# First cross attention with the keys of a head in two halves, its maxima moved by small transfers

## The reference, cut to what matters

```python
q = qkv.reshape(bs * N_HEADS, ch, length)          # 16 heads, ch = 16, 512 queries
k = v = y.reshape(bs * N_HEADS, ch, -1)            # 8192 keys
scale = 1.0 / math.sqrt(math.sqrt(ch))
weight = jnp.einsum('bct,bcs->bts', q * scale, k * scale)
weight = jax.nn.softmax(weight.astype(jnp.float32), axis=-1).astype(weight.dtype)
a = jnp.einsum('bts,bcs->bct', weight, v)
```

## Time and profile before

| what | value |
|---|---|
| median of 3 runs | 1473.07 us (1472.67 to 1474.03) |
| the profiled execution: its own time, its span | 1470.89 us, 1469.1 us |
| PE busy | 1398.5 us, 95% of the span |
| DVE busy | 1164.1 us, 79% |
| ACT busy | 946.8 us, 64% |
| POOL busy | 108.3 us, 7% |
| first cross attention | from the start to 711.4 us |
| second cross attention | 1089.3 to 1205.2 us |

### The profile page before, as it was taken

The page is one execution under the profiler, slowest core; times in us unless marked ns, Lnnn a source line. Parts: engine busy times, 40 slices in busy tenths (PEclk is TensorE's granted clock), DMA queues, the critical chain, the costliest instruction groups (busy, mean ns, idle before and its releaser), DMA issues. The chain is left out here.

```text
span 1469.1 us, 27014 instructions
## 1 busy us (share of the span) xinstructions
PE 1398.5 (95%) x10741; PEld 853.0 (58%) x10741; DVE 1164.1 (79%) x1623; ACT 946.8 (64%) x1754; POOL 108.3 (7%) x99
## 2 busy tenths in 40 slices
PE   3999999999999999999898899999989889999998
PEld 1533333333333333333357899999977764567998
DVE  6999999999999999994577666666667456887665
ACT  0288888888888888889275455554533641785553
POOL 8301111111110011100000000000000000000000
PEclk9999999999999999999999999999999999999999
DMA  7334455553444433445203654555436513104440
GB/s 173 110 48 100 108 162 142 142 133 98 113 91 108 87 98 100 114 73 73 86 1 117 261 205 177 176 196 184 172 148 268 229 65 165 65 2 159 184 180 39
DMA packets 34911, 189.20 MB, mean 129 GB/s; under 512 B 7625, under 2 KB 8049, under 8 KB 22769
## 3 DMA queue, kind: packets, MB, share of 16 engines
q1 hardware_dynamic: 34608, 187.49, 42.3%
q10 hardware_dynamic: 192, 0.20, 0.1%
HBM read 163.23 MB, written 21.27 MB: 126 GB/s over the span
## 5 line engine op out<-in xcount | busy, mean ns | idle before, releaser
L449 DVE TENSOR_REDUCE pm<-bank 128x1 f32<-128x1024 f32 x512 | 618.2, 1223 | 16.3 <-PE bank L541 13.5
L511 ACT ACTIVATE probs<-bank 128x512 f32<-128x512 f32 x1024 | 551.2, 598 | 64.5 <-PE bank L558 6.1
L541 PE MATMUL bank<-kst,qst 50*128 50x512 f32 x1024 | 368.2, 459 | 27.0 <-DMA qst<-qsplit 20.0
L558 PE MATMUL bank<-qst,kst 50*128 50x512 f32 x1024 | 364.2, 446 | 1.6 <-DVE pm L449 0.8
L571 PE MATMUL bank<-probs,vext 128*32 128x256 f32 x3840 | 306.5, 391 | 1.9
L558 PEld LDWEIGHTS bank<-qst,kst 50*128 50x128 f32 x1024 | 150.5, 184 | 207.7 <-ACT probs L511 189.2
L1220 PE MATMUL bank<-e_xhi,e_hi 128*128 128x256 f32 (+1 forms) x784 | 222.4, 284 | 5.0 <-DVE e_lo L1155 4.5
L1220 PE MATMUL bank<-e_xhi,e_lo 128*128 128x256 f32 (+1 forms) x784 | 222.0, 283 | 0.0
L1220 PE MATMUL bank<-e_xlo,e_hi 128*128 128x256 f32 (+1 forms) x784 | 221.9, 283 | 0.0
L571 PEld LDWEIGHTS bank<-probs,vext 128*32 128x32 f32 x3840 | 76.0, 107 | 174.3 <-issue 97.9
L541 PEld LDWEIGHTS bank<-kst,qst 50*128 50x128 f32 x1024 | 148.3, 189 | 42.7 <-DVE pm L449 20.7
(11 more groups left out here) (220 smaller groups left out, 1528.4 us busy)
## 6 DMA issues: line engine op xcount, KB each, us to landing
raw<-wall SPq DMA_DIRECT2D x34, 1536.0 KB, 6.5
kst<-kscratch SPq DMA_DIRECT2D x192, 128.0 KB, 4.3
raw<-wall SPq DMA_DIRECT2D x10, 2304.0 KB, 8.7
kscratch<-ksplit SPq DMA_DIRECT2D x15, 1024.0 KB, 4.3
kraw<-ctx_rows SPq DMA_DIRECT2D x16, 512.0 KB, 4.0
vraw<-ctx_vt SPq DMA_DIRECT2D x16, 512.0 KB, 4.7
ctxT<-ctxT SPq DMA_DIRECT2D x8, 1024.0 KB, 11.7
nat<-ctx_chunks SPq DMA_DIRECT2D x6, 1024.0 KB, 22.2
```

The source lines that it names most:

```text
L449: nc.vector.tensor_reduce(pm[:, h % 2, r % 4, r // 4:r // 4 + 1], bank[:, 2 * (r % 2):2 * (r % 2) + 2, :], AX.XY, ALU.max).then_inc(pre_re ...
L511: nc.scalar.activation(probs[:, (XT * h + n) % PR, :], bank[:, bank_of(h, n), :], ACT.Exp, scale=XSCALE).then_inc(probs_ready, 1)
L541: ins = nc.tensor.matmul(bank[:, 2 * (r % 2) + j, :], qst[64 * j:64 * j + KR, h, tt * P:tt * P + P], kst[64 * j:64 * j + KR, h % 2, c * 51 ...
L558: nc.tensor.matmul(bank[:, bank_of(h, n), :], kst[64 * j:64 * j + KR, h % 2, m * P:m * P + P], qst[64 * j:64 * j + KR, h, :], start=True, ...
```

## The change

- A head's keys are taken in two halves. A half has 16 units and 32 score tiles, and the order of TensorE now runs over 32 halves k instead of 16 heads. After the first half the maximum is that of its keys, after the second that of the whole head (`negmax` reduces `pm` from the start of the head). The extra rows are two for the first half and four for the second, and constant rows (`marks`) in `kst`, loaded once, choose which apply.
- The sums of the first half are multiplied by exp of the difference of the two maxima. The differences come from GpSimd (`mdiff`), the exponential from ScalarE (`weight`); SP stores it to DRAM and loads it back to all partitions (`spread_weight`), and GpSimd multiplies and adds (`weigh`, `sum_o`). For the last head TensorE adds the two in PSUM.
- The four turning matmuls and both copies of rows are gone. VectorE turns `nsplit` in blocks of 32 by 32 (`turn_negmax`, after the first reduction of the next half), and eight small transfers on SP move the rows into `qst` (`stack_negmax`).
- ScalarE copies the sums after its sixth exponential of a half instead of the fifth, and TensorE's first values come half a unit later (FIRST_V).
- In the second cross attention the mask is widened and reduced in eight pieces, and idle matmuls are put before the turned exponentials (12) and before the first values (3).

```diff
-KR = 3 * XC + 2
+KR = 3 * XC
+NS = 2
+XN = NS * XH
-XP = XT // 2
-XG = XT // 4
+XST = XT // NS
+XP = XST // 2
+XG = XST // 4
+FIRST_V = LAGP + 1 + PVLAG
-FIRST_BUSY = 18
+FIRST_BUSY = 4
...
+            def stack_negmax(k):
+
+                sp.wait_ge(negmax_turned, k + 1)
+                for j in range(2):
+                    row = 64 * j + KR + 2 * (k % NS)
+                    for q in range(4):
+                        to = qst[row:row + 2, k // NS, :].rearrange("k (t q c) -> k t q c", t=4, q=4)[:, :, q, :]
+                        sp.dma_start(to.bitcast(F32), nblocks[32 * q:32 * q + 8, k % 2, :]).then_inc(negmax_stacked, 16)
+
+            def spread_weight(h):
+
+                sp.wait_ge(weight_ready, h + 1)
+                sp.dma_start(wscratch[h].rearrange("(p t) -> p t", t=4), weight[:, :]).then_inc(weight_moved, 16)
+                sp.wait_ge(weight_moved, 32 * h + 16)
+                if h > 0:
+                    sp.wait_ge(weighted, h)
+                sp.dma_start(weights[:, :, :].rearrange("p c t -> p (c t)"), wscratch[h].partition_broadcast(P)).then_inc(weight_moved, 16)
...
             for h in range(XH):
+                if h > 0:
+                    if h == 1:
+                        sp.wait_ge(negmax_stacked, 64 + 128)
+                    stack_negmax(NS * h - 1)
                 if h < XH - 1:
                     store_split(h + 1)
                     load_stack(h + 1, 0)
                     load_q(h + 1)
-                    load_stack(h + 1, 1)
...
+                if h > 0:
+                    spread_weight(h - 1)
...
+                stack_negmax(NS * h)
+                if h < XH - 1:
+                    load_stack(h + 1, 1)
+                else:
+                    sp.wait_ge(scores, XST * (NS * h))
+                    for n in range(XHA):
+                        load_nd(n)
...
+            stack_negmax(XN - 1)
+            spread_weight(XH - 1)
             sp.wait_ge(o_stored[0], 16 * XH // 2)
             sp.wait_ge(nd_set, 2)
             load_nd(XH - 2)
...
+            def turn_negmax(k):
+
+                dve.wait_ge(nsplit_step, 2 * k + 2)
+                nc.vector.transpose(nblocks[:, k % 2, :], nsplit[:, k % 2, :].bitcast(F32)).then_inc(negmax_turned, 1)
+
+            for k in range(XN):
+                h, half = divmod(k, NS)
                 for r in range(XP):
-                    if h >= 1 and r == TURN_UNIT:
-                        stack_negmax(h - 1)
+                    if k >= 1 and r == 1:
+                        turn_negmax(k - 1)
...
             for h in range(XH):
+                split_negmax(NS * h)
+                if h < XH - 2:
+                    split(h + 2)
                 if h > 0:
+                    weigh(h - 1)
+                    sum_o(h - 1)
                 if h < XH - 1:
                     values(h + 1)
+                split_negmax(NS * h + 1)
...
-                    if n == 4 and h > 0:
-                        copy_o(h - 1)
+                    if n == 5 and k > 0:
+                        copy_o(k - 1)
+                    if n == 8 and k % NS == 1:
...
+                        nc.scalar.activation(weight[:, :], mdiff[:, k // NS % 2, :], ACT.Exp, scale=XSCALE).then_inc(weight_ready, 1)
...
             def score(k, n):
...
                 if n == 0:
-                    pe.wait_ge(negmax_stacked, 2 * h + 2)
+                    pe.wait_ge(negmax_stacked, 64 + 128 * (k + 1))
...
@@ cross_attention_1
+            keep_busy(g, 12, 5)
             for i in range(MI + 1):
                 if i < MI:
                     turn(i)
+                if i == 1:
+                    keep_busy(g, 3, 7)
...
-                if c == 3:
-                    link(nc.vector.tensor_reduce(okay[:, :], mb[:, :], AX.X, ALU.max))
...
                 if c < MC - 1:
+                    widen_mask(c + 1)
                     cut_rest(c + 2)
+                    link(nc.vector.tensor_reduce(okays[:, c:c + 1], mb[:, 512 * c:512 * c + 512], AX.X, ALU.max))
+                    if c == MC - 2:
+                        link(nc.vector.tensor_reduce(okays[:, c + 1:c + 2], mb[:, 512 * c + 512:], AX.X, ALU.max))
```

More of the change, by code:

```diff
@@ L352, in _ @@
             load_nd(XH - 2)
-            sp.wait_ge(scores, XT * (XH - 1))
-            for h in range(XHA):
-                load_nd(h)
         @block.gpsimd
         def _(pool):
-            for j in range(2):
-                nc.gpsimd.memset(qst[64 * j + 32:64 * j + 34, 0, :].bitcast(F32), 0.0).then_inc(const_set, 1)
-            pool.wait_ge(const_set, 2)
             nc.gpsimd.memset(ident[:, :], 0.0).then_inc(g.ident_ready, 1)
@@ L515, in _ @@
-            copy_o(XH - 1)
+            for k in range(XN):
+                for n in range(XST):
+                    act.wait_ge(scores, XST * k + n + 1)
+                    if n % 4 == 0 and XST * k + n >= PR:
+                        act.wait_ge(pv_done, XG * k + n // 4 + 1 - PR // 4)
+                    nc.scalar.activation(probs[:, (XST * k + n) % PR, :], bank[:, bank_of(k, n), :], ACT.Exp,
+                                         scale=XSCALE).then_inc(probs_ready, 1)
+                    if n == 5 and k > 0:
+                        copy_o(k - 1)
+                    if n == 8 and k % NS == 1:
+                        act.wait_ge(apart, k // NS + 1)
+                        if k // NS > 0:
+                            act.wait_ge(weight_moved, 32 * (k // NS))
+                        nc.scalar.activation(weight[:, :], mdiff[:, k // NS % 2, :], ACT.Exp, scale=XSCALE).then_inc(weight_ready, 1)
@@ L517, in _ @@
+            copy_o(XN - 1)
         @block.tensor
         def _(pe):
-            def turn(h):
-                pe.wait_ge(nsplit_step, 2 * h + 2)
-                if h > 0:
-                    pe.wait_ge(probs_ready, XT * (h - 1) + TURN_AT - 2)
-                for tt in range(4):
-                    ins = nc.tensor.matmul(bank[0:NSW, s_bank(h - 1, TURN_AT), tt * P:tt * P + P], nsplit[:, tt, :], identr[:, :],
-                                           start=True, stop=True)
-                ins.then_inc(negmax_turned, 1)
@@ L544, in pre, with score @@
                     ins.then_inc(pre_scores, 1)
-            def score(h, n):
-                m, j, slot = n // 2, n % 2, place(n)
+            def score(k, n):
+                h, half = divmod(k, NS)
+                m, j, rows = XP * half + n // 2, n % 2, KR + 2 * half + 2
                 if n == 0:
-                    pe.wait_ge(negmax_stacked, 2 * h + 2)
-                if h == XH - 1:
+                    pe.wait_ge(negmax_stacked, 64 + 128 * (k + 1))
+                if k == XN - 1:
@@ L561, in pv, with values_ready @@
-            def pv(h, q, half):
+                        pe.wait_ge(probs_ready, XST * k + n + 1 - len(LAST_BANKS))
+                elif k > 0 or n >= 3:
+                    pe.wait_ge(probs_ready, XST * k + n - 2)
+                nc.tensor.matmul(bank[:, bank_of(k, n), :], kst[64 * j:64 * j + rows, h % 2, m * P:m * P + P],
+                                 qst[64 * j:64 * j + rows, h, :], start=True, stop=True).then_inc(scores, 1)
+            def values_ready(k, q):
+                pe.wait_ge(probs_ready, XST * k + 4 * q + 4)
+                if q == 0:
+                    if k % NS == 0:
+                        pe.wait_ge(v_ready, k // NS + 1)
+                    if k > 0:
+                        pe.wait_ge(o_copied, k)
```

271 lines of the change are left out of this document (129 added, 142 removed).

## The result

| | median | runs | ratio to before, 95% interval |
|---|---|---|---|
| before | 1472.87 us | 1469.38 to 1474.03 | |
| after | 1537.98 us | 1533.91 to 1551.43 | 1.046 (1.040 to 1.052) |

The forecast was 1463.7 us. The profiled execution of the changed kernel took 1539.7 us. Its page shows where: against the kernel before, in which the clock is at full speed in the whole stage but for its end, PEclk stands at 6 to 8 in five of the first twenty slices, the first cross attention, and DVE and ACT fall with it.

The account below looks back on a forecast made before the run. The stage was taken as bound by PE, with DVE 3% behind. Profiled 1470.9 - 7.4 (first cross attention) - 2.0 (second) = 1461.5; the median of the runs is 2.2 higher, so 1463.7 us, range 1453 to 1478.

Parts of the forecast that it names:

- Start, the first `negmax`: Stage start: only 16 units left in front, 18.2 us less, so the first negmax at 39.9 us.
- First loop, "one wait comes in": First loop takes 20.0 us: 19.0 plus 1.0 of wait because GpSimd does values(0) ahead of the first split.
- The way of the maxima, "issued at 1.55 + 7 x 0.59": SP's eight small transfers after negmax: last issued at 5.7, landing at 7.7; first halves wait 0.5 a pair, 7.0 in all.
- SP is free at 21.1 to 21.9: SP's queue, counted from the previous negmax: free 1.4 to 2.2 us after a first half's negmax, taken as 1.9.
- the forecast's own upper bound, 14 x 1.9 = 26.6: First halves' wait for maxima: at most 1.9 us a pair, if the landing takes the median of 4.0, over 14 pairs.
- Rival 2: SP's queue is the new limit and the kernel slower: pairs wait 1.9 us, 19.6 more, 1483 us; chance 0.16.
- Half 30, 2.8 us: Half at k = 30: six nd loads in front of the maxima's transfers add 2.8 us, between 0 and 3.2.
- Thirty halves at 19.67, "I take the values' wait for gone too": Halves after the first loop: 19.67 us each, 590.1 in all, with no turn and no wait for ScalarE's copy.
- rival 3: Slow VectorE turn, or first values still waiting 0.3 us in 32 places: 9 more, 1473 us, no change; chance 0.14.
- The end, -7.4: After the last negmax: VectorE waits for head 14's sums, 43.7 us instead of 51.16; stage ends 7.4 us earlier.
- Second cross attention, -2.0: Mask reduced in pieces removes PE's 2.6 us wait, pieces delay the maximum 0.6; net -2.0 us, between -3 and 0.

Follow-up runs that it names:

- experiment 6: Kernel of experiment 1 with SP's transfers reordered at the stage's start and end, and VectorE taking heads 0 to 7 first; 1464.42 us, 0.999 of before.
- experiment 10: Kernel of experiment 6 with fewer transfers ahead of the first maxima, their split and the last maxima's transfers earlier, 8 idle matmul pairs before the first score; 1459.26 us.
- experiment 1: Changed kernel with the weight's store and load moved behind the first half's eight small transfers on SP's queue; 1483.68 us, 1.008 of before.
- experiment 4: Changed kernel with pairs of idle matmuls (20, 24 or 5) on two row groups ahead of each first half's first score; 1522.95 us, 1.034 of before.
- experiment 5: Kernel of experiment 1 with last values between two scores, sums copied after the fifth exponential, next first values at their own unit's end; 1488.57 us, 1.010.
- experiment 7: Kernel of experiment 6 with both last quarters of a half's values one unit earlier and sums copied after the fifth exponential; 1466.08 us, 0.995 of before.
- experiment 8: Kernel of experiment 6 with ScalarE copying from a fixed SBUF tile, TensorE waiting for no copy, sums not computed; 1453.68 us, 0.990 of before.
- experiment 9: Kernel before the change with only the edits of the second cross attention; 1468.90 us, 0.997 of before.
- experiment 2: Changed kernel with the late scores one unit later (LAGP 8 for 7); 1528.49 us, 1.037 of before.

## Why the prediction was wrong

- **Start, the first `negmax`:** right (39.9 for 40.98).
- **First loop, "one wait comes in":** wrong. GpSimd's wait was there, 0.58 for 1.0, but the step left out what the four transfers of constant rows do to SP's queue. In the changed kernel they occupy SP for 6.28 us at the place where the first maxima are due, the raw keys' issue behind them another 2.64, and the eight started 5.8 after `negmax`. TensorE waited 6.1 us for the rows, and (1 - 0.72) / 0.5 x 30.98 = 17.3 us of the loop are at 1.2 GHz. Experiments 6 and 10 give 10 of the 11.0 back.
- **The way of the maxima, "issued at 1.55 + 7 x 0.59":** right for second halves: they start 1.5 after `negmax`, take 5.2 to 5.3, and cost almost nothing. For first halves the failed step is "SP is free at 21.1 to 21.9". The last link of that sum was right: from the issue of the raw keys to that of the weight's load it allowed 4.1 to 4.9, and 3.9 to 5.3 were measured. What it had too short stands ahead of it: the split store was to land at 10.3, and the key loads behind it started at 10.7 to 13.4, so the raw keys were issued at 17.3 to 19.9 instead of 16.6. The eight started 1.5 to 5.4 us after `negmax`, in nine of the fourteen first halves later than the 2.2 of the forecast, and one every 0.66 instead of 0.59. That gives 16.9 us of idle matmuls in eleven places, up to 3.9 at once, instead of 0.5 in each of fourteen.
- **The missing term:** this is the step that failed by most. No step priced TensorE's clock; every wait was charged at its own length. The waits in halves 4, 8, 12 and 22 were followed by stretches at 1.2 GHz, 7 us long after half 8's ((1 - 0.87) / 0.5 x 26.46) and 31 after half 22's, and half 12, with 18.6 us of it and 2.9 idle, came out 10 longer. The clock is about 30 of the 49.0 (30.5 by experiment 1, at least 24.8 by experiment 4); the 17 of idle time lie within the forecast's own upper bound, 14 x 1.9 = 26.6. Rival 2 had the right mechanism, and at 0.16 too small a chance; even its 1483 had no clock in it.
- **Half 30, 2.8 us:** the mechanism was right (six loads of sums in front), the size was not: 8.6 of wait, and the clock on top. The eight were issued from 702.96 to 708.14, on time; TensorE could start on them at 717.96, 16.5 after `negmax`, where the forecast had 10.6.
- **Thirty halves at 19.67, "I take the values' wait for gone too":** wrong by 0.35 a half, rival 3's case, now 31 times instead of 16. The forecast saw the 0.3 in a head and thought that another place of the copy would remove it. Neither of the two other orders tried (experiments 5 and 7) removes it; taking the bank's hand-over away (experiment 8) does. Our reading is that one unit without values, or with two, breaks the step of TensorE and VectorE, which are only two pairs of banks apart and are both nearly full. So halving the keys, which doubles the hand-overs, eats 31 x 0.35 - 16 x 0.3 = 6 of the 16 x 0.5 = 8 us that the turns gave.
- **The end, -7.4:** the chain was right, head 14's sums behind the last weight; VectorE stood 18.14 us for them, and the end took 46.2 for 43.7, because their load landed 7.6 us after its issue and not 4.3. Ordering it otherwise (experiment 6) is worth 10 more.
- **Second cross attention, -2.0:** right. The stage takes 1.9 less in the changed kernel and 2.0 in experiment 9, whose median is 4.1 lower for a reason that no trace shows.

What stays open is what decides whether a wait is followed by low clock: half 10 idled 2.0 us and stayed at 2.4 GHz, half 4 idled 1.3 and did not; in experiment 2 half 16 idled 1.8 and stayed, and half 14 idled 2.3 and did not.

## What to carry to other kernels

Price a wait of TensorE at its length, and ask what a stretch of low clock behind it would add: of the five waits here between 1.3 and 3.9 us, four were followed by 7 to 31 us at 1.2 GHz, which cost 30 us in all. A kernel at 98% busy has no room to win that back. Before small transfers are put on a queue in a loop, list what stands ahead of them at each turn, and keep every "store, wait for its landing, load" behind what is urgent. Splitting a loop in two doubles its hand-overs: look for the bank or tile that one engine must empty before another may go on.

## What the runs showed of the hardware

- Idle matmuls in the waits of TensorE hold the clock in most cases and not in all: with six single ones on 48 rows twelve of fourteen first halves stayed at 1.00 and two fell (half 4 was granted 0.68 with 28.87 of its 29.57 us busy), with five pairs on two row groups thirteen stayed and one fell to 0.93; without any, in the changed kernel, ten stayed and four fell.
- A low clock outlasts the wait in front of it: half 23 begins at 1.2 GHz, TensorE is busy in all of its 26.10 us, and (1 - 0.76) / 0.5 x 26.10 = 12.5 of them are at 1.2 GHz.
- Eight transfers of 1 KB in 128-byte pieces from SBUF to SBUF cost 5.28 / 8 = 0.66 us each to issue. In e12_quiet_start the eight of one half go out from 404.43 to 409.71, and the first score that needs them is loaded at 410.74 with no more than the usual 0.41 of idle time, so the last, issued at 409.1, landed within 1.7. What they cost here is the 5.28 us of issue; their small pieces show no wait.
- Four transfers of four rows each backed up the queue. In e6_start_and_end the four `marks` transfers of 64 KB came first, and the one of 512 KB behind them took 4.03 us to issue and 14.1 to land:

```profile
L277 SPq DMA_DIRECT2D vraw<-ctx_vt x1: 4030/4030/4030, 27.5 to 27.5; - x1
DMA to landing us min/median/max: 14.1/14.1/14.1
```

The Trainium skill, DMA: Bandwidth & Descriptors, section Why a DMA increments its semaphore by 16 and not by 1, says that a transfer runs on the largest number of engines, up to 16, that divides the slowest dimension of both its sides; for four rows that is four. The trace shows the delay, and not the engines.
